# Order of ScalarE's decays and TensorE's state sums in layer 0 of a two-layer decoder, and two more state products on GpSimd

## The reference, cut to what matters

```
# per channel (256), state (16) and token, for each of 4 sequences
dA    = exp(delta * A)
state = state * dA + (delta * u) * B_t
y_t   = sum over the states n of state[n] * C_t[n]
...
q, k  = layernorm_unit(rotate(q)) * 256, layernorm_unit(rotate(k)) ; v = layernorm_unit(v)
probs = softmax(tanh(q k^T / sqrt(32) / 30) * 30, masked to the window)
x     = x + (probs v) Wo
```

## Time and profile before

| | us |
|---|---|
| median of 3 runs | 897.97 (896.33 to 901.73) |
| the profiled execution | 897.47, its span 895.7 |
| VectorE busy | 687.4 (77%) |
| TensorE busy | 748.8 (84%) |
| ScalarE busy | 490.8 (55%) |
| GpSimd busy | 353.7 (39%) |

### The profile page before, as it was taken

The page is one execution under the profiler, slowest core; times in us unless marked ns, Lnnn a source line. Parts: engine busy times, 40 slices in busy tenths (PEclk is TensorE's granted clock), DMA queues, the critical chain, the costliest instruction groups (busy, mean ns, idle before and its releaser), DMA issues.

```text
span 895.7 us, 12576 instructions
## 1 busy us (share of the span) xinstructions
PE 748.8 (84%) x4016; PEld 576.6 (64%) x4016; DVE 687.4 (77%) x1230; ACT 490.8 (55%) x1062; POOL 353.7 (39%) x247
## 2 busy tenths in 40 slices
PE   6770479877799986799999999999846899999997
PEld 2240356554433565677877887887734689999996
DVE  4897689889879887898899899899967454444443
ACT  1744458650336603577777877779834254444442
POOL 1001355552331553232333333333534286666663
PEclk9785659998899997899999999999978899999999
DMA  4341123345020212011211111212400344433331
GB/s 174 123 162 35 71 94 128 109 142 222 0 77 0 60 59 94 13 36 36 60 36 36 60 37 37 59 36 60 143 1 0 101 162 141 139 138 139 139 128 48
DMA packets 28886, 74.66 MB, mean 83 GB/s; under 512 B 3632, under 2 KB 6336, under 8 KB 28448
## 3 DMA queue, kind: packets, MB, share of 16 engines
q1 hardware_dynamic: 28384, 71.51, 23.7%
q10 hardware_dynamic: 448, 2.49, 0.8%
HBM read 72.55 MB, written 1.44 MB: 83 GB/s over the span
## 4 chain that ended last, share of the span: by engine, by line
PE 53%; DVE 19%; issue 12%; ACT 11%; POOL 2%; DMA 1%; POOLq 0%; DVEq 0%; ACTq 0%; SPq 0%
PE ps L1862 6%; PE ps L1863 6%; PE ps L1864 6%; PE ps L1827 4%; PE ps L1706 4%; DVE hS L1032 4%; PE ps L1815 3%; PE ps L1748 2%; PE ps L1749 2%; PE ps L1750 2%; PE ps L1797 2%; PE ps L1796 2%; PE ps L1510 2%; DVE H L1089 2%; PE ps L1786 1%
## 5 line engine op out<-in xcount | busy, mean ns | idle before, releaser
L420 POOL TENSOR_TENSOR hS<-hS,BCb 128x512 f32<-128x512 f32 x64 | 82.3, 1290 | 137.7 <-issue 68.2
L1462 DVE SCALAR_TENSOR_TENSOR arena<-ps,arena 128x1024 f32<-128x1024 f32 x32 | 39.2, 1224 | 102.9 <-ACT arena L898 93.1
L443 POOL TENSOR_TENSOR hS<-hS,BCb 128x1024 f32<-128x1024 f32 x23 | 56.2, 2441 | 107.9 <-DVE ps L1024 93.8
L508 POOL TENSOR_TENSOR MHl<-arena,MHh 128x1024 fp32r<-128x1024 f32 x34 | 81.7, 2404 | 17.6 <-ACT MHh L901 17.6
L1491 PE MATMUL ps<-ident,hS 128*128 128x128 f32 x256 | 41.2, 317 | 53.1 <-POOL hS L443 46.6
L1862 PE MATMUL ps<-Wh,MHh 128*128 128x256 f32 x272 | 77.8, 286 | 6.2 <-POOL MHl L508 6.2
L1062 DVE TENSOR_TENSOR_SCAN hS<-dA,ps 128x512 f32<-128x512 f32 x64 | 78.1, 1220 | 2.2
L1863 PE MATMUL ps<-Wl,MHh 128*128 128x256 f32 x272 | 77.5, 285 | 0.0
L1864 PE MATMUL ps<-Wh,MHl 128*128 128x256 f32 x272 | 77.5, 285 | 0.0
L1491 PEld LDWEIGHTS ps<-ident,hS 128*128 128x128 f32 x256 | 34.0, 163 | 63.8 <-POOL hS L443 53.0
L505 POOL TENSOR_TENSOR Wl<-WB,Wh 128x512 fp32r<-128x512 f32 x34 | 47.2, 1391 | 64.2 <-ACT Wh L882 64.2
(11 more groups left out here) (241 smaller groups left out, 2127.6 us busy)
## 6 DMA issues: line engine op xcount, KB each, us to landing
BCb<-bc_dram SPq DMA_DIRECT2D x32, 512.0 KB, 3.8
BCb<-bcq_dram SPq DMA_DIRECT2D x64, 256.0 KB, 3.2
arena<-gate_dram SPq DMA_DIRECT2D x32, 512.0 KB, 3.6
WB<-in_we SPq DMA_DIRECT2D x34, 256.0 KB, 2.7
WB<-in_wqkv SPq DMA_DIRECT2D x1, 3072.0 KB, 13.0
WA<-in_wo ACTq DMA_DIRECT2D x1, 2048.0 KB, 7.6
WA<-in_ffn SPq DMA_DIRECT2D x1, 1408.0 KB, 7.4
pkb<-in_pk SPq DMA_DIRECT2D x2, 698.0 KB, 4.7
```

The source lines that it names most:

```text
L420: gp.tensor_tensor(h, h, qbc(q)[:, 1:2, :].broadcast_to([P, DT, S]), ALU.mult).then_inc(s["c_ready"], 1)
L443: gp.tensor_tensor(h, h, BCb[g % SB_LOADS][:, 1:2, :].broadcast_to([P, DT, HALF]), ALU.mult).then_inc(s["c_ready"], 1)
L508: gp.tensor_tensor(MHl[:, p, :], MH[p], MHh[:, p, :].bitcast(F32), ALU.subtract).then_inc(s["m_lo"], 1)
```

## The change

Four things are edited, all in layer 0; what is computed stays the same.

1. In ScalarE's list, steps_to(7) moves from behind the squares to before them: decays 4 to 7 are issued ahead of the wait for the centred q, k and v. Decays 8 and 9 follow the squares, decay 10 stands ahead of the copies of the transposed groups, decay 11 between copies 4 and 5. Before, decays 8 to 13 followed the first unit's exp.
2. In TensorE's list, state sum 6 moves ahead of the scores of unit 0 and state sum 7 behind them; both came after the first product with v.
3. For units 0 and 1 acc_to stops one step earlier.
4. POOL_STEPS ends at 28 instead of 26: C of steps 27 and 28 goes to GpSimd, their B products to PSUM, and conv(2) waits for scan 28.

```diff
-POOL_STEPS = range(4, 27)
+POOL_STEPS = range(4, 29)
...
             d_u(1)
+            steps_to(7)
             act.wait_ge(s["rope0_rot"], 1)
             sc.activation(SQ0, Q0.rearrange("p t n -> p (t n)"), ACT.Square).then_inc(s["rope0_sq"], 1)
-            steps_to(7)
+            steps_to(9)
             act.wait_ge(s["rope0_done"], 1)
...
+            steps_to(10)
             for i in range(8):
+                if i == 5:
+                    steps_to(11)
                 act.wait_ge(s["tr0_mm"], i + 1)
...
-            step = iter(range(6, LAYER_STEPS))
+            step = iter(range(8, LAYER_STEPS))
...
+            acc(6)
             s0(0)
+            acc(7)
             for u in range(UNITS0):
...
-                acc_to(AT0_AT[u] - 2)
+                acc_to(AT0_AT[u] - (3 if u < 2 else 2))
```

## The result

The changed kernel takes 886.72 us (median of 4 runs, 883.9 to 889.23) against 897.69 us (896.33 to 901.73) in the same comparison. The ratio is 0.987, with a 95% interval of 0.9826 to 0.9913, so it is faster by 8 to 16 us. Two later comparisons with the same kernel gave 0.9853 both times (intervals 0.9831 to 0.9874 and 0.9824 to 0.9883). The forecast was 885.7, with a range of 882.5 to 890.5. The profiled execution's span is 885.2 us, against 895.7 before.

A forecast was written before the change was run, and what follows sets the result against it. VectorE was taken to bound layer 0's scan stage, idling mostly for ScalarE's decays. Terms -4.37 - 6.52 - 1.8 + 0.4 = -12.3 us took 897.97 to 885.7 us, range 882.5 to 890.5.

The forecast's parts named there:

- Decays 4 to 7: ScalarE's decays issued ahead of the squares: scan 4 starts at 75.74 instead of 80.11, -4.37 us.
- Decays 8 to 11 with edit 2: Scan 8's 6.52 us wait for its decay vanishes, with state sums 6 and 7 made in time: -6.52 us.
- Over 3 us: VectorE's product 10, had TensorE kept its old order: its forecast wait for state sum 6.
- Divisions 0 and 1: VectorE's waits for TensorE in units 0 and 1 fall from 2.62 us to 0.8 together: -1.8 us.
- the first three terms: Layer 0's scan: -4.37 (decays 4 to 7), -6.52 (decays 8 to 11), -1.8 us (divisions 0 and 1).
- the 113 us: Time from about which TensorE was assumed to run at its upper clock level, 2.4 GHz.
- Rival (c): Not faster: TensorE's low clock holds on through the units, 898 to 920 us; chance 0.03.
- The tail: C of steps 27 and 28 on GpSimd: two VectorE products become two waits, 0 to +1.7 us, taken as +0.4.
- The upper bound: Tail at 1.2 GHz: sum 27 and transpositions take 3.7 us, VectorE's copy starts at 202.8; cost +1.7 us.
- Those of being right: No decay waits at scans 4, 8; table load near 59; product 12 near 114.2; C 27 2.35, C 28 about 4.3 us.
- The copy's wait: VectorE's copy of the heads' output in the tail waits about 2.3 us for TensorE.
- the signs of being wrong: Products waiting in steps 9-12, division waits above 2 us, clock 0.50 beyond unit 2, over 1 us change behind layer 0.

## Why the prediction was right, point by point

**Decays 4 to 7, -4.37.** Product 6 moved from 96.07 to 92.75, which is -3.32, or -4.36 without the 1.04 us of the later start. The squares and the reduction behind them kept their cover.

**Decays 8 to 11 with edit 2, -6.52.** Scan 8 moved from 111.33 to 101.53: -9.80, or -10.84 in all, -6.48 beyond the first term. Product 12 came at 115.29; 114.2 was forecast and 1.04 is the start. The claim that edit 2 protects this term was the most fragile one, and the kernel with ScalarE's edit alone showed it: without edit 2 nearly all of the second term is gone. "Over 3 us" for the wait at product 10 was on the low side, it was 5.75: product 10 was due at 106.11 and not 106.7, and sum 6 began at 109.80 rather than near 109 and ran at the lower clock level.

**Divisions 0 and 1, -1.8.** They do not wait at all, so the term is -2.62: division 1 moved from 135.23 to 122.62, -12.61, or -13.65 without the start, against the 12.7 of the first three terms. The clock rose earlier than the 113 us that I had assumed; the windows of TensorE's clock in the changed kernel (length, busy, clock, DMA share, GB/s):

```profile
99.00:101.00 2.00, 2.00 (x11) 0.50 0.09 31
101.00:103.00 2.00, 2.00 (x14) 0.64 0.75 248
103.00:105.00 2.00, 1.84 (x17) 1.00 0.04 14
```

TensorE had done nothing but sum 5 and the transpositions since 96.5, and it was at 1.00 from 103 us on. It did not stay there: behind a wait of 1.96 us for VectorE, ahead of unit 1's transposition at 119.39, the granted clock was 0.50 from 120 to 122 us. No division waited behind it.

By a rule that the prediction weighed, transposes do not count as work for the clock (the Trainium skill, TensorE: Matmul & The Clock Gate, Part 4: PE-mode transpose). The windows above show otherwise: 0.50 and then 1.00, behind transposes alone. Rival (c) did not come.

**The tail, +0.4.** It cost 1.26 us, inside the 0 to 1.7 that the prediction held open. Taking 0.4 was the mis-sized choice. TensorE, idle for 3.41 us ahead of sum 27, came back at the lower level, and the copy waited 3.3 to 3.9 us in the five profiles with edit 4 and an unchanged tail instead of 2.3. The upper bound, worked out with that level, was the case that occurred. GpSimd's C 27 in 2.34 and C 28 in 4.33 us are as forecast.

**What the sum did not have.** From unit 9 on the first profile gains another 1.5 us: division 9 waits 0.17 us where it waited 1.70. The sum had no term for this, and how much of it is the change's is open: the last section shows a short and a long wait in one and the same kernel. Up to product 27 the shift is 189.88 - 175.73 = 14.15 us, 15.2 without the start; C 29 is 12.89 earlier, and layer 0's gate 230.04 - 217.22 = 12.82. Of these, 10.5 arrive at the end of the span. One is lost at once: layer 0's feed-forward ends 11.84 earlier. TensorE's clock is 0.80 from 200 to 260 us there, where it was 0.89 in the same work before (212 to 272); that this is the cause is not shown. The rest goes in the loop over the experts of layer 1's feed-forward. Its 32 gated products, with the first and the last start, in the first profile and then in a later one of the same kernel:

```profile
L1466 DVE SCALAR_TENSOR_TENSOR arena<-ps,arena x32: 1224/1225/1225, 699.3 to 871.2; 128x1024 f32<-128x1024 f32 x32
...
L1466 DVE SCALAR_TENSOR_TENSOR arena<-ps,arena x32: 1223/1224/1225, 697.4 to 867.8; 128x1024 f32<-128x1024 f32 x32
```

That is 171.9 and 170.4 us; the kernel before took 711.3 to 881.7, which is 170.4. Ten of the fourteen profiles have 170.4 and four 171.9, and kernels with and without the change are among both, so this loss belongs to the execution and not to the change. The same holds for the whole stretch from the gate to the end: 668.0, 666.5 and 665.1 us in the three profiles of the changed kernel, 665.7 in the kernel before, 664.3 to 668.2 over all fourteen.

The terms mis-sized or left out are -0.8 (divisions), +0.9 (tail), -1.5 (unit 9) and +2.3 (behind layer 0). They nearly cancel, and with the later start of 1.04 us they make the profiled -10.5 out of the forecast -12.3. That the profile and the median both come within about 2 us of the forecast is in part luck: the mechanism and the two large terms were right, but the last two of these four differ between executions of one kernel.

**The signs.** Those of being right came at steps 4 and 8, at the table load (58.35), at product 12 and at GpSimd's C 27 and C 28. The copy's wait (3.70 for about 2.3) and the span (885.2 for about 883.4) did not. Of the signs of being wrong, a change behind layer 0 of more than a microsecond did appear, as told above. In the later profile of the changed kernel two more appeared, a wait of a division of 3.07 us and a granted clock of 0.50 from 151 to 159 us, far beyond unit 2. The prediction had taken that from unit 2 on TensorE keeps ahead of VectorE; behind the first half's transpositions it does not always.

## What to carry to other kernels

Where an engine that was idle for microseconds ends another's wait, look at the order of its list first. Before pricing the repair, though, walk the moved steps through every queue: here the second half of the gain existed only together with a reordering on a third engine. Moving work off the bounding engine is worth its full time only if nobody behind it waits for the slower result. Here two products of 1.23 us and a wait of 2.25 us became waits of 3.7 and 2.25 us. Moving the transpositions in front of a sum that they did not need, and changing the home of one operand, turned that loss into a further gain of over 5 us.

## What the runs showed of the hardware

**Behind two short gaps the clock fell in some executions and not in others.** TensorE idles 1.62 us before and 0.83 us behind the first half's transpositions. Over the twelve profiles with these two gaps (the kernel before, the changed one in its first profile, and ten of the experiments) the next product with v took 1.95 to 1.98 us in eight and 1.08 in four. In the kernels without edit 2 it was the longer time in all four profiles, in those with it in four of eight: too few to say whether the change makes the fall rarer. One and the same kernel, the changed one, showed both; what decides it is open. First profile, then a later one:

```profile
152.47 1.08 PE L1626 MATMUL ps<-WB,arena 128*64 128x256 f32 x8 [0.83 <-ACT hT L726]
...
156.00 0.18 DVE L1192 RECIPROCAL rden<-ps 128x4 f32<-128x4 f32 x1 [0.17 <-PE ps L1636]
```

```profile
150.81 1.98 PE L1626 MATMUL ps<-WB,arena 128*64 128x256 f32 x8 [0.83 <-ACT hT L726]
...
157.24 0.18 DVE L1192 RECIPROCAL rden<-ps 128x4 f32<-128x4 f32 x1 [3.07 <-PE ps L1636]
...
162.21 0.18 DVE L1192 RECIPROCAL rden<-ps 128x4 f32<-128x4 f32 x1 [1.00 <-PE ps L1636]
```

That is 3.9 us of waits between two executions of one program. It does not show in these two spans, 885.2 and 885.4 us, since the later profile had reached the rotation 1.64 us earlier and was 1.5 us shorter behind the gate. How long the level stays down differs as well: in the later profile two products with v took 1.98 us, and division 9 waited 3.07 us. In the kernel before and in four of the experiments only one did, and division 9 waited 1.61 to 1.80 us. In the two profiles with a sum in the second gap the level held both times; two are too few to call it a rule. A single wait was enough elsewhere: the granted clock went from 1.00 to 0.50 behind one of 2.64 us (edit 3 undone, sum 10) and behind one of 1.96 us (the changed kernel, at 119.39).

**GpSimd beside a scan.** A product of GpSimd took 2.34 to 2.37 us beside a scan with one input in PSUM and 4.33 or 4.34 beside one with both inputs in SBUF. Edit 4 alone shows it: C of step 26, which runs beside scan 27, took 4.34 us while step 27's B product lay in SBUF and 2.35 us with it in PSUM (at 177.08 in the changed kernel). Doing the same for step 29 (with the transpositions moved too) shortened C 28 from 4.33 to 2.34 us and the wait for it from 2.25 to 0.26 us; the two edits of the tail were not run apart, but each has its own wait in the trace.
